# Gated cross-attention and mixture-of-experts block on one core: another order of weight pieces and turned rows, one product for Wq and Wk, and later constants

## The reference

```python
def adjacency(h, adj_raw, Wq, Wk, gamma_raw):      # h: context (4, 512, 128), adj_raw: layernorm(x)
    Q, K = heads(h @ Wq.T), heads(h @ Wk.T)        # 4 heads, summed over below
    sim = einsum('bhnd,bhmd->bnm', Q, K) / (sqrt(32) * 4)
    threshold = 153rd largest of each row of sim
    A = sigmoid(sim) * (sim >= threshold)
    A = (A + swapaxes(A, -1, -2)) * 0.5
    return (1 - sigmoid(gamma_raw)) * adj_raw + sigmoid(gamma_raw) * A

def ffn(x):                                        # 2048 rows of 512
    shared = (silu(g) * y) @ shared_dw.T           # y, g = split(x @ shared_gw.T), 704 wide
    scores = sigmoid(x @ gate_w.T)                 # 8 experts, 2 chosen by scores + bias
    out = sum over the 2 experts of w_e * ((silu(g_e) * u_e) @ down_w[e].T)   # 352 wide
    return shared + out

x = x + tanh(g_xattn) * adjacency(ctx, layernorm(x), ...)
x = x + tanh(g_ffn) * ffn(layernorm(x))
```

## Time and profile before

| | |
|---|---|
| median of 3 runs | 587.41 us (586.65 to 587.45) |
| profiled execution | 586.68 us |
| its span | 584.8 us |
| TensorE busy | 504.6 us (86%) |
| VectorE busy | 339.8 us (58%) |
| ScalarE busy | 256.3 us (44%) |
| GpSimd busy | 214.9 us (37%) |
| bytes moved | 57.50 MB, 98 GB/s |

### The profile page before, as it was taken

How to read it: one execution, slowest core, us unless ns; L and a number is a source line. 1 busy time by engine, 2 the same in 40 slices (tenths; PEclk the granted TensorE clock), 3 DMA queues, 4 the chain that set the end, 5 groups by cost and what they waited for, 6 DMA issues and landing times.

```text
span 584.8 us, 10606 instructions
## 1 busy us (share of the span) xinstructions
PE 504.6 (86%) x3141; PEld 281.4 (48%) x3142; DVE 339.8 (58%) x719; ACT 256.3 (44%) x468; POOL 214.9 (37%) x229
## 2 busy tenths in 40 slices
PE   2456399598998899879877999999999999999992
PEld 0134244244444444434354566666666666666660
DVE  0698469767788778868995576433333333333330
ACT  1492756728674866554451265332222222223221
POOL 2201324830267116812543034434433433443422
PEclk9866679898999999989999999999999999999997
DMA  4411141323225222440225689554444454454433
GB/s 143 159 46 48 31 141 38 113 77 123 77 76 151 109 91 58 117 154 21 84 58 166 198 234 245 86 97 73 78 97 76 76 87 88 72 88 91 72 49 42
DMA packets 28597, 57.50 MB, mean 98 GB/s; under 512 B 3664, under 2 KB 3920, under 8 KB 28560
## 3 DMA queue, kind: packets, MB, share of 16 engines
q1 hardware_dynamic: 19824, 36.60, 19.9%
q0 software_dynamic: 8736, 20.45, 19.6%
HBM read 37.90 MB, written 19.14 MB: 98 GB/s over the span
## 4 chain that ended last, share of the span: by engine, by line
PE 54%; DVE 22%; ACT 10%; issue 6%; DMA 4%; POOL 2%; SPq 0%; DVEq 0%; POOLq 0%; ACTq 0%
PE py L1063 13%; PE pg L1043 12%; PE pu L1044 12%; PE pt_bank L839 3%; DVE w L1168 3%; PE pa L1053 2%; DVE work L1318 2%; ACT w L596 2%; PE py L926 2%; DVE w L1260 2%; PE pg L903 2%; DVE pa L1198 2%; PE pu L903 2%; DMA stage<-in_weights 1%; DVE w L1202 1%
## 5 line engine op out<-in xcount | busy, mean ns | idle before, releaser
L1043 PE MATMUL pg<-w,x_t 128*128 x468 | 140.8, 313 | 0.0
L1044 PE MATMUL pu<-w,x_t 128*128 x468 | 140.7, 313 | 0.0
L557 POOL DMA_INDIRECT out<-rows,idx x39 | 61.8, 1585 | 142.2 <-ACT rows L779 129.2
L1063 PE MATMUL py<-w,work 128*128 x351 | 82.1, 379 | 0.7 <-DVE work L1525 0.7
L903 PE MATMUL pg<-w 128*128 128x512 f16 x288 | 79.1, 392 | 3.6 <-DVE work L1318 3.6
L769 ACT ACTIVATE work<-pg 128x352 f32<-128x352 f32 x39 | 18.0, 462 | 129.9 <-PE pu L1044 129.9
L903 PE MATMUL pu<-w 128*128 128x512 f16 x240 | 67.6, 392 | 0.0
L596 ACT ACTIVATE w<-stage 128x544 f16<-128x544 f32 x80 | 50.8, 648 | 27.5 <-DMA stage<-in_weights 24.2
L502 POOL TENSOR_TENSOR w<-stage,w 128x544 f16<-128x544 f32 x42 | 55.3, 1332 | 11.5 <-DVE w L1285 10.0
L516 POOL TENSOR_TENSOR work<-work 128x512 f16<-128x512 f32 x20 | 24.1, 1205 | 95.4 <-ACT work L678 94.5
L1514 DVE SCALAR_TENSOR_TENSOR work<-pu,work 128x352 f32<-128x352 f32 x39 | 20.4, 524 | 64.4 <-ACT work L769 64.4
(11 more groups left out here) (222 smaller groups left out, 777.3 us busy)
## 6 DMA issues: line engine op xcount, KB each, us to landing
stage<-in_weights SPq DMA_DIRECT2D x80, 272.0 KB
w<-in_x SPq DMA_DIRECT2D x4, 1024.0 KB, 6.4
xn_rows<-w SPq DMA_DIRECT2D x16, 256.0 KB, 2.0
out<-w SPq DMA_DIRECT2D x16, 256.0 KB, 2.1
w<-in_ctx_t SPq DMA_DIRECT2D x4, 256.0 KB, 3.1
out<-rows,idx POOLq DMA_INDIRECT x39, 4.7
work<-xn_rows,idx POOLq DMA_INDIRECT x20
xg<-xn_rows,idx POOLq DMA_INDIRECT x19
```

The lines of the kernel that those rows point to most:

```text
L557: pool.indirect_dma_start(out=out, out_offset=bass.IndirectOffsetOnAxis(ap=idx[:, t:t + 1], axis=0), in_=rows[:, t % 2, :], in_offset=None ...
L1043: pe.matmul(pg[p][:, 0:H], lhs, w[:, item, half, at:at + H], start=begin, stop=end)
L1044: mm = pe.matmul(pu[p][:, 0:H], lhs, w[:, item, half, at + H:at + 2 * H], start=begin, stop=end)
L1063: mm = pe.matmul(py[:, :], hid_t[:, p, part * JC + j, :], w[:, item, half, at:at + C], start=(j, part, half) == (0, 0, 0), stop=(j, part) ...
```

## The change

Six parts, named by what the code does.

- The first loads are Wq and Wk (no longer transposed), then the context of batch 0. TensorE multiplies `Wq^T Wk` once, ScalarE copies it to `wqk`, and each `project` is one product with it instead of two; the scores multiply its result with the context itself, which has a buffer of its own now. `keep_qk` copies one tile instead of two.
- The constants `cst` (three hyperbolic tangents and six small VectorE operations) and the router weights' fp16 parts are made by ScalarE behind `keep_scores(0)` and by VectorE behind `score_stats(0)`, and not at the start. GpSimd makes `guess(0)` ahead of them.
- `FIRST` is 8 instead of 10, and the slots hold (2, 2, 2, 2, 2, 4) pieces in batch 0 and (0, 1, 2, 2, 0, 8) in batches 1 and 2, instead of (0, 1, 2, 2, 2, 3) in each and eight more in batch 3, which has none now. In steps 1 to 3 the pieces stand ahead of the high and low parts of the hidden rows, in the others behind. The first down product waits for pieces step by step instead of for all sixteen.
- TensorE makes the low parts of pieces 4 and 5 ahead of the turn of batch 0's attention; ScalarE's list follows.
- Turned rows: in batch 0 VectorE copies turned tile 0 between the low parts of rows 1 and 2, ScalarE turns tile 1 ahead of the score copies and tile 3 ahead of the hyperbolic tangents. In the others VectorE copies shared row 2 and turned tile 0 ahead of the score statistics.
- Batch 3: ScalarE's high part of step u - 1 comes behind silu u. On VectorE shared row 1 goes ahead of pieces 4 to 7 of item 6, and pieces 6 and 7 behind shared row 2. The loads of x have two semaphores instead of one.

```diff
@@ -20,10 +20,8 @@
 SLOTS_STEP = 4
 SLOTS_STEPS = TOPK * TILES // SLOTS_STEP
 BY_PE = 6
-FIRST = 10
-SLOT_PIECES = (0, 1, 2, 2, 2, 3)
-PER_PERIOD = sum(SLOT_PIECES)
-LAST_PIECES = (2, 2, 2, 2, 0, 0)
+FIRST = 8
+SLOT_PIECES = ((2, 2, 2, 2, 2, 4), (0, 1, 2, 2, 0, 8), (0, 1, 2, 2, 0, 8))
 KEEP = int(SEQ * 0.3)
 UP_W = KC * 2 * H
...
         hot = attn_buf(2 * SEQ + TPB * SEQ // 2)
-        q_t, k_t = hot[:, 0:SEQ], hot[:, SEQ:2 * SEQ]
-        ctx_b = q_t
+        q_t, ctx_b = hot[:, 0:SEQ], hot[:, SEQ:2 * SEQ]
         junk = hot[:, 2 * SEQ:].bitcast(F16).rearrange("p (i c) -> p i c", i=TPB)
         masked = junk.rearrange("p i c -> p (i c)").bitcast(F32).rearrange("p (i c) -> p i c", i=2)
...
@@ -275,16 +274,12 @@
         def low_uses(k):
             return [j for j in range(k) if low_pair(j) == low_pair(k)]
 
-        def period_pieces(b):
-            k = FIRST + b * PER_PERIOD
-            slots = []
-            for count in SLOT_PIECES if b < BATCHES - 1 else LAST_PIECES:
-                slots.append([(j // CHUNKS, j % CHUNKS) for j in range(k, k + count)])
-                k += count
-            return slots
-
         def pieces_by(b, u):
-            return FIRST + b * PER_PERIOD + sum((SLOT_PIECES if b < BATCHES - 1 else LAST_PIECES)[:u])
+            return FIRST + sum(sum(slots) for slots in SLOT_PIECES[:b]) + sum(SLOT_PIECES[b][:u]) if b < len(SLOT_PIECES) else LATE * CHUNKS
+
+        def slot_pieces(b, u):
+            begin = pieces_by(b, u)
+            return [(k // CHUNKS, k % CHUNKS) for k in range(begin, begin + SLOT_PIECES[b][u])]
 
         def late_pieces(t):
...
@@ -357,9 +352,9 @@
                 after(sp, y_sb, b * TPB + i + 1)
                 sp.dma_start(out_tiles[:, b * TPB + i:b * TPB + i + 1, :], xbs[b % 2][:, i:i + 1, :]).then_inc(sh_st[i % 2], 16)
 
+            sp.dma_start(wq_s, wq).then_inc(wqk_ld, 16)
+            sp.dma_start(wk_s, wk).then_inc(wqk_ld, 16)
             load_context(0)
-            sp.dma_start(wq_s, wq_t).then_inc(wqk_ld, 16)
-            sp.dma_start(wk_s, wk_t).then_inc(wqk_ld, 16)
             load_x(0)
             sp.dma_start(gcol[:], gates.rearrange("(a n) -> a n", a=1).partition_broadcast(P)
...
@@ -515,8 +508,9 @@
                     return
                 pool.tensor_tensor(hid_tb[:, u, 1, :], hb[:, u % 2, :], hid_tb[:, u, 0, :], ALU.subtract).then_inc(hlo_sb, 1)
 
+            guess(0)
+            pool.wait_ge(cst_ok, 1)
             base_scalars(0)
-            guess(0)
             row_scalars(0, 0)
             row_scalars(0, 1)
...
                 for u in range(UPS):
                     if u == TPB - 1:
                         base_scalars(b + 1)
-                    shared_low(b, u)
-                    for piece in slots[u]:
-                        low_piece(*piece)
+                    if 0 < u < TPB:
+                        for piece in slot_pieces(b, u):
+                            low_piece(*piece)
+                        shared_low(b, u)
+                    else:
+                        shared_low(b, u)
+                        for piece in slot_pieces(b, u):
+                            low_piece(*piece)
...
             act.activation(warm[:], rows[:, 0, 0:1], ACT.Silu).then_inc(warm_ok, 1)
-            act.wait_ge(small_ld, 16 * SMALL)
-            act.activation(cst[:, 0:2], gcol[:, 0:2], ACT.Tanh).then_inc(cst_act, 1)
-            act.activation(cst[:, 2:3], gcol[:, 2:3], ACT.Tanh, scale=0.5).then_inc(cst_act, 1)
-            act.activation(gw[:, :, 0, :], gw_f, ACT.Copy, scale=W_SCALE).then_inc(gw_hi, 1)
+            act.wait_ge(wqk_mm, 1)
+            act.activation(wqk[:], pt_bank[:, 0:D], ACT.Copy).then_inc(wqk_sb, 1)
 
             def high_piece(item, n):
...
             def keep_qk(b):
                 after(act, sim_mm, b * TPB)
-                after(act, qk_mm, b * 2 + 2)
-                for n, dst in enumerate((q_t, k_t)):
-                    act.activation(dst, score_banks[n][:, :], ACT.Copy).then_inc(qk_sb, 1)
+                after(act, qk_mm, b + 1)
+                act.activation(q_t, score_banks[0][:, :], ACT.Copy).then_inc(qk_sb, 1)
 
             def keep_scores(b):
...
@@ -682,6 +675,12 @@
                     keep_qk(b + 1)
                 for i in range(TPB):
                     normalised(b, i)
+                if b == 0:
+                    rows_turned(b, 1)
+                    keep_scores(b + 1)
+                    rows_turned(b, 3)
+                    score_tanh(b + 1)
+                    return
                 if more:
                     keep_scores(b + 1)
...
 
             keep_qk(0)
             keep_scores(0)
+            act.wait_ge(small_ld, 16 * SMALL)
+            act.activation(cst[:, 0:2], gcol[:, 0:2], ACT.Tanh).then_inc(cst_act, 1)
+            act.activation(cst[:, 2:3], gcol[:, 2:3], ACT.Tanh, scale=0.5).then_inc(cst_act, 1)
+            act.activation(gw[:, :, 0, :], gw_f, ACT.Copy, scale=W_SCALE).then_inc(gw_hi, 1)
             for n in range(ROUNDS):
...
             high_piece(0, 4)
             low_from_banks(3)
             high_piece(0, 5)
+            low_from_banks(4)
             high_piece(0, 6)
+            low_from_banks(5)
+            high_piece(0, 7)
             keep_qk(1)
-            low_from_banks(4)
-            high_piece(0, 7)
-            low_from_banks(5)
-            for k in range(CHUNKS, FIRST):
-                high_piece(k // CHUNKS, k % CHUNKS)
             scores_and_rows(0, True)
...
+                    if 0 < u < TPB:
+                        for piece in slot_pieces(b, u):
+                            high_piece(*piece)
                     shared_high(b, u)
                     if u == 0:
                         count(b + 1, 3)
-                    for piece in slots[u]:
-                        high_piece(*piece)
+                    if u == 0 or u >= TPB:
+                        for piece in slot_pieces(b, u):
+                            high_piece(*piece)
                 scores_and_rows(b + 1, more)
 
...
             for u in range(UPS):
                 shared_silu(BATCHES - 1, u)
-                shared_high(BATCHES - 1, u)
-                for piece in period_pieces(BATCHES - 1)[u]:
-                    high_piece(*piece)
+                if u:
+                    shared_high(BATCHES - 1, u - 1)
+            shared_high(BATCHES - 1, UPS - 1)
             for s in sh_st:
...
             pe.wait_ge(wqk_ld, 32)
+            pe.matmul(pt_bank[:, 0:D], wq_s, wk_s, start=True, stop=True).then_inc(wqk_mm, 1)
+            pe.wait_ge(wqk_sb, 1)
 
...
                     after(pe, hid_sb, (shared + 1) * UPS)
-                for n, m in enumerate((wq_s, wk_s)):
-                    pe.matmul(score_banks[n][:, :], m, ctx_b, start=True, stop=True).then_inc(qk_mm, 1)
+                pe.matmul(score_banks[0][:, :], wqk[:], ctx_b, start=True, stop=True).then_inc(qk_mm, 1)
 
             def scores(b, i):
-                after(pe, qk_sb, (b + 1) * 2)
+                after(pe, qk_sb, b + 1)
                 if i >= 2:
                     after(pe, x1_made, b * TPB - TPB + i - 1)
-                pe.matmul(score_banks[i][:, :], q_t[:, i * P:(i + 1) * P], k_t, start=True, stop=True).then_inc(sim_mm, 1)
+                pe.matmul(score_banks[i][:, :], q_t[:, i * P:(i + 1) * P], ctx_b, start=True, stop=True).then_inc(sim_mm, 1)
 
...
                 bank_ = down_bank(b, i)
-                if b == 0 and 0 in pieces and i == 0:
-                    pieces_ready(HALVES * CHUNKS)
...
                     half, at = shared_down_at(u)
+                    if b == 0 and i == 0:
+                        pieces_ready(half * CHUNKS - (-(at + C) // CHUNK_W))
                     if u == MIXED:
...
             for i in range(TPB):
                 scores(0, i)
             pe.wait_ge(const_ok, 2)
-            low_pieces(0, RING)
+            low_pieces(0, RING + 1)
             missed_rows(0)
+            low_pieces(RING + 1, BY_PE)
             after(pe, w_lo[RING - 1], 1)
             turn_attention(0)
             project(1, None)
-            low_pieces(RING, RING + 1)
             for i in range(TPB):
                 scores(1, i)
-            low_pieces(RING + 1, BY_PE)
             for i in range(TPB):
                 turn_batch(0, i)
...
@@ -1284,22 +1277,25 @@
                         o.wait(made)
                     dve.tensor_tensor(xnr[:, i, C:2 * C], xn[:, i % 2, :], xnr[:, i, 0:C], ALU.subtract).then_inc(xn_lo, 1)
 
-                for i in (0, 2):
-                    if i and b == 0:
-                        after(dve, xn_lo, b * TPB + i)
-                    made = [exact(i), exact(i + 1)] if b == 0 else [None, None]
-                    low_rows(i, made[0])
-                    low_rows(i + 1, made[1])
-                after(dve, up_mm, b * UPS)
-                if shared is None:
+                if b == 0:
+                    made = [exact(0), exact(1)]
+                    low_rows(0, made[0])
```

(18 more changed lines are left out.)

44 lines of the change are left out of this document (20 added, 24 removed).

## The result

The changed kernel takes **569.67 us** (568.29 to 570.08) beside 587.03 us of the kernel before on the same chip: ratio 0.9704, 95% interval 0.968 to 0.9728. Timed again with later experiments it took 570.28 us, ratio 0.9736 (0.9709 to 0.9763). It is 17 us faster; 29 were forecast, and 569.7 lies 0.7 us above the range of 554 to 569.

A forecast was written before the change was run, and what follows sets the result against it. Time was to be won in TensorE's holes before the expert stage, argued from five waits. 4.0 + 9.1 + 6.3 + 1.5 + 5.7 + 2.4 = 29.0 us; 586.7 - 29.0 + 0.7 = 558.4 us, forecast 558.5, range 554 to 569.

The forecast's parts named there:

- Periods 1 and 2, 1.5 us: Batches 1 and 2: down product wait goes, eight pieces end as row scalars are due; 0.4 each plus 0.7 once.
- signs of being wrong: Whole kernel: silu or row scalars wait longer, x lands late, or TensorE runs more at 1.2 GHz; no size given.
- Rival (b): Batches 1 and 2: burst of eight costs in both, pieces at 1.65 us and slower ring; 564.5 us; 10%.
- Batch 0's period, 6.3 forecast: Batch 0: first down product waits some 0.6 instead of 6.04 us, next step starts sooner; 6.3 us gained.
- The copy order: Ends of batch periods: turned row 0 copied ahead of score statistics, logits 0.7 us sooner.
- Rival (a): Period 0 ScalarE-bound: TensorE waits for hidden rows about 1.2 us in five slots, 6 us; 564.5 us; 15%.
- Start, 4.0 forecast: Kernel start: single Wq-Wk product and projection, constants behind scores; search and masks 4.0 us earlier, range 2.5 to 4.9.
- Turned rows of batch 0, 9.1: Before batch 0's first gate product: pieces 8 and 9 leave, the load wait goes; 9.1 us gained, range 7.5 to 10.
- Router's batch, 5.7: Batch 3: eight pieces leave, VectorE is no longer held up, TensorE's waits for hidden rows go; 5.7 us gained.
- Tail, 2.4: Before the expert stage: shared row 1 ahead of pieces 4 to 7 removes the 2.41 us wait; bounds 0 and 2.4.

The follow-up runs named there:

- second profile: A second profile of the unaltered changed kernel: first gate product at 62.99 us, periods 0 to 2 of 63.47, 64.24 and 64.44 us.
- e9: Changed kernel with three buffers for the hidden rows instead of two, so silu(q) waits for the low half of q-3: 564.17 us, ratio 0.9624.
- e5: Changed kernel with GpSimd making the last four of the last slot's eight lows behind the row scalars (batches 1 and 2): 562.03 us, ratio 0.9601.
- e1: Changed kernel with the high and low parts of the hidden rows ahead of the slot's pieces in every slot: 568.25 us, ratio 0.9687.
- e4: Changed kernel with the context of batch 0 loaded ahead of Wq and Wk: 568.99 us, ratio 0.9706.
- e10: Changed kernel with e5, e4 and e1 together (e1's hidden halves first in slots 1 to 3): 559.03 us, ratio 0.9537.
- e14: e10 with the third buffer for the hidden rows added: 560.97 us, ratio 0.9582.
- e15: Changed kernel with VectorE's old order ending periods 1 and 2: score statistics, shared row 2, then turned row 0: 571.82 us, ratio 0.9753.
- e7: Kernel before with only the start's parts and two semaphores for x; pieces and rows as before: 583.53 us, ratio 0.9968.
- e12: Changed kernel with VectorE's old tail order, pieces 4 to 7 of the late item ahead of shared row 1: 574.18 us, ratio 0.9797.

## Why the prediction was wrong

The direction was right, the sum 11 us too high. **The step that failed is "Periods 1 and 2, 1.5 us"**, in it the start of the eight pieces at 176.6 and their end just when the row scalars are due: measured -6.9, which is 8.4 of the 10.7 us by which the trace misses the sum of 29.0. By the second profile it is -9.0, and 10.5 of 11.9.

- **Periods 1 and 2.** The prediction said: GpSimd starts the eight pieces at 176.6 and ends them near 188.1, just when the row scalars are due. Their length was right, the start was not: 38.7 us from the gate instead of 34.0. Part of this stood in the trace of the kernel before, GpSimd's timeline:

```profile
176.10 1.15 POOL L516 TENSOR_TENSOR work<-work 128x512 f16<-128x512 f32 x1
177.21 2.84 POOL L502 TENSOR_TENSOR w<-stage,w 128x544 f16<-128x544 f32 x2
180.42 1.19 POOL L512 TENSOR_TENSOR work<-work 64x512 f16<-64x512 f32 x1 [0.37 <-POOL w L502]
```

  low(4) ends at 177.25, after the 176.6 of the forecast, and low(5) is still to come. Without the two pieces of slot 4 (2.84 us) low(5) ends at 178.8, and the pieces can start some 36.5 from the gate: 2.5 of the 4.7 us. Another 1.4 is silu(5)'s wait for low(3), by e9 beside the second profile. I had counted only the two pieces that leave slot 4, and not what a low half behind x scalars and pieces holds up through the two hidden buffers. VectorE was not 2.3 us ahead either: its x updates start 36.6 from the gate, before at 35.6. So no slack was left, and the scalars came 4.5 us late.

  A second thing was missing from this term and from the whole sum: a price for TensorE's clock, which the prediction named only among its signs of being wrong. Of the 6.9 us, 4.3 are more idle time of TensorE and 2.5 more busy time, for products begun at a clock of 0.50 where it had been 0.72 (period 1); in the second profile it is 4.3 and 4.7 of 9.0.

  The runs price the lateness in two parts: the order of the row scalars (e5: periods 2.3 and 3.7 shorter than in the first profile, 2.2 and 6.1 than in the second) and the wait of silu(5) (e1 with e5 and e4: 1.5 and 1.0 more). Both gone, the periods are 60.57 and 57.39, 1.7 below before's in sum, about the forecast 1.5. Rival (b) named the burst, with 6 us for both periods and 10%; against the forecast 1.5 it cost 8.4 to 10.5. Its reason, every piece at 1.65 us and a slower ring, was not the one: the pieces took what was forecast.
- **Batch 0's period, 6.3 forecast, 3.4 measured.** The x updates were to start 36.5 from the gate and started at 38.96; before it was 37.05. The same wait is part of it: with the third buffer (e9) they start at 37.15 and the period is 1.5 us shorter. With the hidden halves first (e1, e10, e14) silu(5) does not wait there either, and nothing is gained. The waits of the down product are 1.47 us in sum, not 0.6. The copy order was given 0.7 here and 0.7 once in periods 1 and 2; e15 shows 1.5 and 1.1 in the periods, but 1.0 to 1.5 in the total, so the sum of the two terms stands. Rival (a), TensorE waiting in five slots, fell: it waits once, 1.86 us.
- **Start, 4.0 forecast; the search came 2.4 us sooner.** "The same bytes land by about 9.4" was wrong for this order: the context is third in the queue, and TensorE waits until 11.49. With the context first (e4) the projection starts at 10.68 and waits only for the copy, and the search comes at 22.40, 4.1 sooner than before the change. The product was 0.77 (0.6 taken), the copy 0.28 (0.3).
- **Turned rows of batch 0, 9.1.** Right: 11.7 less 2.4 is 9.3 (10.2 by the second profile), and no load of a weight piece stands in the chain ahead of 63.9. The start alone (e7) moved the gate by 5.9, so the two parts overlap: part of what I gave to the rows the start alone gets, as ScalarE then reaches the rows sooner too.
- **Router's batch, 5.7.** The mechanism was right: all waits of TensorE are gone, and the stretch is 6.4 us shorter (47.30 and 40.90). TensorE's own 41.3 us, taken as the floor, became 40.8. Six pieces put back cost 4.6. The Trainium skill (SBUF — State Buffer, section "SBUF: two separate sides") describes an exclusive lock between a GpSimd operation that reads SBUF and a VectorE operation with two inputs there. The trace agrees: the four x updates take 5.57 us under GpSimd's operations and 2.74 alone.
- **Tail, 2.4.** Undersized: what is left of the 10.0 us is 3.6. Of TensorE's two waits before, the forecast counted one, 2.41 us, and not the one ahead of it (timeline of the kernel before):

```profile
318.41 0.61 PE L839 MATMUL pt_bank<-ident,work 128*128 128x128 f16 x8 [0.78 <-issue]
```

  With the old order in the changed kernel the two waits cost 5.3 us (e12), as the products behind them then run at the lower clock. In the kernel before they did not (12 in 2.77 us), with only the start changed they did (12 in 4.35, e7): which of the two an execution gets is not foreseen by the length of the wait. Router's batch and tail together gave 1.9 us more than forecast and hid that much of the miss: without it the time would lie not 0.7 but 2.6 us above the range.

Left open: where the other 1.2 us of e7 go, and why e4's 1.7 us is under one in the total, if that is not noise. No wait in the traces accounts for either.

## What to carry to other kernels

When work is gathered into a burst, ask what stands behind it in the same engine's order, and put the small operations that another engine waits for ahead of it: here that was 7 us for the same work. Part of such a gain can be TensorE's clock, so look at busy time and granted clock of a stretch beside its waits before you call a wait the whole cause. Before moving a piece ahead of a low half, follow the buffer that this half frees, not only the product that reads it. When a forecast gives a burst a new start, add up all that its engine still has to do ahead of it: here the old trace alone put it 2.5 us later. A slack of 2 us that a forecast uses up to the last is a reason to price the case in which it does not suffice.

## What was not expected of the hardware

- One wait of nearly the same length cost TensorE its clock in two traces and not in a third: 2.47 us, then 12 products in 4.39 us at 0.61 (e12), and 2.46 us, then 12 in 4.35 us (e7); 2.41 us, then 12 in 2.77 us at 1.00 (before). Ahead of the wait all had done the same, 0.61 us of turning behind another wait of 0.91, 0.69 and 0.78 us. Why the clock fell in two of them is not shown.
- A wait of 2.23 us ahead of period 2 went with 5 us at a clock of 0.50 behind it; with 0.79 us in its place the clock was 1.00 (e5).
- A load of 256 KB, issued third at 5.94 us, behind two of 64 KB and ahead of one of 1 MB, is not used until 11.49; the profile names nothing that ends this wait, and e4 points at the load. Issued first, at 5.07, it no longer ends the wait, and the projection starts at 10.68, 0.37 us behind the copy. The product of Wq and Wk then starts 2 us later, at 9.54 instead of 7.54.
- Where they meet, GpSimd's piece and VectorE's x update both get longer: the piece from 1.22 to 1.67 us, the update from 0.7 to between 1.65 and 1.71 (period 1 of the changed kernel). So VectorE pays 1.0 us and GpSimd 0.45 for a meeting.
